# Carrying stores over a block's end, reloading split tokens from DRAM, and gathers in groups: a three-stage decoder layer on one core

## Chip, core and metric

The kernel runs on one core of a Trainium2 chip. The metric is device time in microseconds: the median of several executions of the kernel before is set against that of the changed kernel on the same chip. An execution with the profiler on is recorded beside them.

## What is computed

One decoder layer with three residual parts over x of 8 × 256 tokens with 256 channels, in float32.

```python
x = x + mamba2(layernorm(x))                # W_in: z, x: 4096 channels each (64 heads of 64), B, C: 128 each, dt: 64
x = x + cross_attention(layernorm(x), ctx)  # 16 heads of 128, 4 key heads, 64 context tokens, q and k RMS-normed
x = x + experts(layernorm(x))               # 8 experts of 640, 2 per token, and 2 shared ones

# mamba2: xBC = silu(conv4(x, B, C)); dt = softplus(dt + bias); dA = dt * A
#         y = scan(C, B, dA, x * dt) + D * x; return rmsnorm(y * silu(z)) * norm_w @ W_out.T
# experts: s = sigmoid(x @ router.T); the two largest of s, normalized to sum 1, weigh two of 8
#          w_e * (silu(x @ wg.T) * (x @ wu.T)) @ wd.T, and the shared experts are added unweighted
```

## The kernel before

The 2048 tokens are 16 tiles of 128, in 4 groups of 512. The large products are float32 operands split into a high part, rounded to the type that TensorE multiplies at full rate, and a low part that holds the rest; a product is three matmuls (high by high, low by high, high by low), so each tile of tokens and each weight needs a high part (a copy by ScalarE) and a low part (a subtraction by DVE or POOL).

The program is a row of blocks. In each the five engines run instruction lists written by hand, with semaphores between them; at a block's end all engines meet, and the next begins.

`mamba_prepare` (0 to 91 us of work): layer norm, transposes of x into the buffers called `pair` (`pair_hi`, `pair_lo`), dt, the decay sums, B and C with their convolution. Beside it the weights w_xz go through in 16 pieces j: SP loads a piece (512 KB), ScalarE makes the high part (`w_high(j)`), DVE (j < 7) or POOL the low part, SP stores both to DRAM (`w_split`, 1 MB). The parts lie in a ring of four buffers, so `w_high(j)` waits for the store of j − 4. The loop over the 8 tiles m of the B/C convolution carries `w_high` along:

```python
tanh(m)
if m + 9 < NJ:      # NJ = 16
    w_high(m + 9)
```

SP waits for all 16 stores before the block ends. The decay sums `a_by_head` are stored in four transfers behind piece 10. The first weights (`w_first`) and decays are already in place for the scan.

`mamba_scan` (97.6 to 967): 128 iterations, 4 groups of tokens by 32 tiles of channels. Each loads split weights again from DRAM, projects x and z (`x_proj`, `z_proj`, six matmuls of 128x512 each), and does the scan, the gate and the output projection for neighbouring iterations. At n = 8 SP issues the attention's loads.

`cross_attention_phase` (to 1282.8): 8 sequences b. Sequence b's scores, softmax (`exp` on ScalarE, the rest on DVE) and attend run beside the q projections of b + 1 (`q_pair` on TensorE, `q_out` on ScalarE: four ACTIVATEs which free the PSUM bank of the q_pair two further on), and beside layer norm, transposes, high and low parts (`f_high`, `f_low`; `x2_hi`, `x2_lo`) and router logits of b − 1. The parts of x2 are one pair of small buffers, used for the logits alone. `pair` holds wq's parts here.

`ffn_phase`: `dense(0)` is the first shared expert over all tokens: 4 units u of 512 tokens by 5 tiles of the hidden width, 20 steps k of `gate_up` (12 matmuls of 128x512), ScalarE's `silu`, DVE's `h` and its low part (`to_lo`), `down(u)`. Beside its steps runs the routing on DVE: `logits_in`, `scores`, `ranks`, ties, choices, at k = 5 TensorE's `counts_before`, then places; POOL scatters token rows by expert to DRAM in groups of 8 indirect transfers, each group waiting for the one before. `f_xT_hi`, `f_xT_lo` are the tokens' transposed parts again: `transposes`, `xT_high`, `xT_low` for 16 tiles, four ahead of the first gate_up, the last two tiles (14, 15, whose logits are made here by `late_logits`) at k = 0, the others at k = 2, 3, 7, 8 and 12. Then come 39 tiles of sorted rows (1390.6 to 1630), and `dense(1)`, the second shared expert, in which POOL gathers the results (32 indirect transfers, two a tile; a tile's buffer is free once an earlier tile is combined) and DVE's `combine(n)` adds tile n at the steps k = 4 to 19.

## Time and profile before

| | |
|---|---|
| median of the runs | 1717.1 us (3 runs, 1716.67 to 1723.58) |
| the recorded execution | 1731.19 us |
| its span | 1729.4 us, 28895 instructions |
| mean granted TensorE clock | 0.973 |
| TensorE busy (matmul) | 1614.9 us, 93% |
| DVE / ScalarE / POOL busy | 1311.0 / 1222.5 / 601.3 us |
| DMA | 220.30 MB, mean 127 GB/s |

Times of the trace are from the span's start. The recorded execution has 1.8 us outside its span. "Idle before" and its releaser stand in brackets behind an instruction. PE is TensorE, ACT ScalarE, SP the engine that issues most transfers. The prefixes p_, m_, a_ and f_ of names stand for the four stages.

### The profile page before, as it was taken

The numbers are of one execution on the slowest core, as the hardware profiler recorded it, in microseconds if no ns is written. First come the engines' busy times: TensorE is split into PE (matmuls) and PEld (weight loads), VectorE is DVE, ScalarE is ACT, GpSimd is POOL, SyncE is SP. The second block draws the span as 40 slices with busy tenths as digits, with TensorE's granted clock in tenths as the row PEclk, the third lists the DMA queues.
The fourth block names the chain that finished last, engine by engine and source line by source line (L and its number), as shares of the span: only waits on it lengthen the run. The fifth ranks groups of instructions, "written<-read, shape, count | busy, mean of one in ns | idle before, by whom it ended". The sixth has DMA issues, their size and how long they took to land. (4 is left out here: it accounts for less than half of the span.)

```text
span 1729.4 us, 28895 instructions
## 1 busy us (share of the span) xinstructions
PE 1614.9 (93%) x9892; PEld 1289.2 (75%) x9892; DVE 1311.0 (76%) x2048; ACT 1222.5 (71%) x2531; POOL 601.3 (35%) x469
## 2 busy tenths in 40 slices
PE   4479999999999999999999999999968999999989
PEld 3257777777777777777777677777757889999868
DVE  7859999999999999999999756765557533333345
ACT  5669999999999999999999566665524333444321
POOL 1413343434343434343433321111112563336450
PEclk9679999999999999999999999999979999999989
DMA  8956444444444444444442100000132323222221
GB/s 309 393 212 246 162 155 170 148 163 154 170 149 162 155 170 150 169 147 171 148 170 98 55 1 1 1 1 1 47 105 84 127 103 110 93 91 96 79 86 43
DMA packets 74268, 220.30 MB, mean 127 GB/s; under 512 B 8848, under 2 KB 29584, under 8 KB 72464
## 3 DMA queue, kind: packets, MB, share of 16 engines
q1 hardware_dynamic: 68464, 192.38, 31.1%
q0 software_dynamic: 5664, 26.09, 4.3%
q8 instruction: 84, 1.38, 0.3%
q14 instruction: 56, 0.46, 0.1%
HBM read 184.62 MB, written 33.82 MB: 126 GB/s over the span
## 5 line engine op out<-in xcount | busy, mean ns | idle before, releaser
L607 POOL TENSOR_TENSOR m_gT<-m_gy,m_zs 128x512 f32<-128x512 f32 x128 | 166.7, 1302 | 537.5 <-DVE m_gy L769 537.5
L728 DVE SCALAR_TENSOR_TENSOR m_xc<-banks,k_cw,m_xc 128x510 f32<-128x510 f32 (+2 forms) x384 | 285.4, 743 | 21.1 <-ACT m_xc L647 12.1
L868 PE MATMUL m_ps_out<-k_won,m_gT 128*128 128x256 f32 x1024 | 242.3, 379 | 3.6 <-POOL m_gT L607 2.0
L825 PE MATMUL banks<-pair_hi,m_wxz 128*128 128x512 f32 x680 | 243.8, 409 | 0.5 <-DMA m_wxz<-w_split 0.5
L740 DVE TENSOR_TENSOR m_mat<-m_mat,k_cbm 128x768 f32<-128x768 f32 x256 | 232.5, 950 | 2.0 <-ACT m_mat L668 2.0
L868 PEld LDWEIGHTS m_ps_out<-k_won,m_gT 128*128 128x128 f32 x1024 | 193.6, 189 | 36.6 <-POOL m_gT L607 3.3
L856 PE MATMUL m_ps_y<-m_mat,m_xdt 128*64 128x256 f32 (+1 forms) x2048 | 194.7, 332 | 0.0
L668 ACT ACTIVATE m_mat<-m_mat 128x1536 f32<-128x1536 f32 x128 | 188.5, 1473 | 0.1
L856 PEld LDWEIGHTS m_ps_y<-m_mat,m_xdt 128*64 128x64 f32 x2048 | 126.8, 136 | 80.0 <-issue 42.3
L659 ACT ACTIVATE m_mat<-m_a_all,k_cum 128x256 f32<-128x256 f32 x340 | 170.7, 502 | 0.0
L618 POOL TENSOR_TENSOR m_g_sum<-m_g_sum,m_g_sq 128x512 f32<-128x512 f32 x124 | 163.2, 1316 | 5.2 <-ACT m_g_sq L674 5.1
L825 PEld LDWEIGHTS banks<-pair_hi,m_wxz 128*128 128x128 f32 x680 | 128.8, 189 | 29.5 <-DMA m_wxz<-w_split 1.2
L2331 PE MATMUL f_gu<-f_room,f_gT_hi 128*128 x468 | 141.3, 363 | 2.4 <-issue 2.4
L2184 DVE TENSOR_TENSOR f_h<-f_silu,f_gu 128x256 f32<-128x256 f32 (+1 forms) x117 | 44.1, 377 | 129.4 <-PE f_ps_hT L2341 107.1
L825 PE MATMUL banks<-pair_lo,m_wxz 128*128 128x512 f32 x340 | 135.4, 398 | 0.0
L825 PE MATMUL banks<-pair_hi,k_w_first 128*128 128x512 f32 x344 | 127.2, 410 | 7.5 <-PEq L73 6.6
L661 ACT ACTIVATE m_mat<-m_a_all,k_cum 128x128 f32<-128x128 f32 x340 | 134.0, 394 | 0.0
L2254 PE MATMUL f_gu<-f_xT_hi,f_room 128*128 128x512 f32 x320 | 109.0, 415 | 11.8 <-ACT f_silu L1904 5.6
L647 ACT ACTIVATE m_xc<-banks,logits,k_cw 128x512 f32<-128x512 f32 x128 | 98.4, 768 | 13.2 <-PE banks L825 13.2
L1093 POOL TENSOR_TENSOR a_q_r<-a_q_ve,a_neg_half 128x32 f32<-128x32 f32 x8 | 43.4, 5429 | 176.8 <-DVE a_q_ve L1280 176.8
L1937 ACT ACTIVATE f_silu<-f_gu 128x256 f32<-128x256 f32 (+1 forms) x117 | 40.9, 349 | 88.0 <-PE f_gu L2331 88.0
L769 DVE SCALAR_TENSOR_TENSOR m_gy<-m_xs,logits,m_ps_y 128x512 f32<-128x512 f32 x128 | 95.5, 746 | 8.5 <-PE m_ps_y L856 0.2
(305 smaller groups left out, 3695.9 us busy)
## 6 DMA issues: line engine op xcount, KB each, us to landing
m_wxz<-w_split SPq DMA_DIRECT2D x85, 512.0 KB, 3.3
m_a_all<-a_by_head SPq DMA_DIRECT2D x85, 512.0 KB, 4.3
k_w_first<-w_split SPq DMA_DIRECT2D x43, 512.0 KB, 3.4
k_a_first<-a_by_head SPq DMA_DIRECT2D x43, 512.0 KB, 4.3
w_split<-p_w_hl SPq DMA_DIRECT2D x16, 1024.0 KB, 9.9
raw<-in_w_gate_up POOLq DMA_DIRECT2D x9, 1280.0 KB, 6.8
raw<-in_w_xz SPq DMA_DIRECT2D x16, 512.0 KB, 7.9
raw<-in_w_down POOLq DMA_DIRECT2D x9, 640.0 KB, 7.9
```

Of the source, the lines that this page charges most:

```text
L607: pool.tensor_tensor(gT[:, n % 2, :], gy[:, n % 2, :], zs[:, n % 2, :], ALU.mult).then_inc(g_done, 1)
L618: pool.tensor_tensor(g_sum[:, g % 2, :], g_sum[:, g % 2, :], g_sq[:, n % 2, :], ALU.add)\
L659: act.activation(mat[:, u, h, b * TRI:b * TRI + SEQ], a_all[u][:, h, b * SEQ:(b + 1) * SEQ], ACT.Relu, bias=cum[:, t, head:head + 1], scal ...
L661: last = act.activation(mat[:, u, h, b * TRI + SEQ:(b + 1) * TRI], a_all[u][:, h, b * SEQ + P:(b + 1) * SEQ], ACT.Relu, bias=cum[:, t + 1, ...
L668: act.activation(mat[:, n % 3], mat[:, n % 3], ACT.Exp, scale=-1.0).then_inc(exp_done, 1)
L728: dve.scalar_tensor_tensor(out=out[:, :, k:], in0=ps[:, :, 0:SEQ - k], scalar=cw[:, c, TAPS - 1 - k:TAPS - k], in1=out[:, :, k:], op0=ALU. ...
L740: dve.tensor_tensor(mat[:, u, h, :], mat[:, u, h, :], cbm[:, g * BG:(g + 1) * BG, :].rearrange("p b t -> p (b t)"), ALU.mult)\
L825: last = pe.matmul(ps[:, :], w, a, start=m == 0, stop=m == len(terms) - 1)
L856: last = pe.matmul(ps_y[h * HD:(h + 1) * HD, b * SEQ + at:(b + 1) * SEQ], xdt[:, 2 * b + half, h * HD:(h + 1) * HD], mat[:, u, h, b * TRI ...
L868: last = pe.matmul(ps_out[:, q * HID:(q + 1) * HID], gT[:, n % 2, q * P:(q + 1) * P], won[:, c, :], start=c == 0 and q % 2 == 0, stop=c == ...
L2254: last = pe.matmul(bank[n % 2][:, :], w, a, start=m == 0, stop=m == len(terms) - 1)
L2331: last = pe.matmul(ps_gu[m % 4][:, 0:2 * (i1 - i0)], a, w, start=q == 0, stop=q == len(terms) - 1)
```

## The change

1. `mamba_prepare`: the semaphores of the stores live on into the scan. The block's end waits for pieces 0 to 13; SP waits for the last two in the scan at n = 8, POOL before its first product. Piece 15 is split into a part of `raw`, and its high part waits for the low part of an earlier piece in place of a store. In the loop over m tanh(5) and tanh(6) stand ahead of `w_high(14)`, tanh(7) ahead of `w_high(15)`. The four stores of `a_by_head` go one each behind pieces 8 to 11; DVE's `w_low(0)` and `w_low(1)` come among the layer norm's tiles. At the scan's start `z_proj(0)` is ahead of `x_proj(1)`, `tanh_x` ahead of `decays`, `silu_x(0)` ahead of `matrices(0)`.
2. Attention: `q_out(b+1, 2)` is ahead of `exp(b, 0)`. The parts x2 of b = 0 to 5 are stored to DRAM (12 stores of 256 KB), those of b = 6 are written straight to `pair`, and after the last q_pair SP loads the stored ones into `pair` (2 × 1.5 MB). In the experts `pair` takes the place of `f_xT`; only tiles 14 and 15 are transposed there, TensorE and ScalarE wait for the reload, and `late_logits` stands behind the k = 1 gate_up.
3. Gathers: group g of 8 waits until group g − 1 has landed; the combines from tile 4 on come one step later, the last two together.

```diff
+        last_hl = raw[:, 0:2 * CH * XZ].bitcast(F32R).rearrange("p (c s m) -> p c s m", c=CH, s=2)
...
+        def hl(j):
+            if j == NJ - 1:
+                return last_hl
+            return w_hl[:, (0, 1, 3, 2)[j % RING]]
...
-                if j == NJ - 6:
+                if NJ - 8 <= j < NJ - 4:
                     sp.wait_ge(aT_done, 2)
-                    for q in range(TPG):
+                    for q in (j - NJ + 8,):
...
-            for u in range(RING):
-                sp.wait_ge(w_stored[u], 16 * len(range(u, NJ, RING)))
+            sp.wait_ge(w_stored[0], 16 * (NJ // RING))
+            sp.wait_ge(w_stored[1], 16 * (NJ // RING))
+            sp.wait_ge(w_stored[2], 16 * (NJ // RING - 1))
+            sp.wait_ge(w_stored[3], 16 * (NJ // RING - 1))
...
-                if j >= RING:
+                if j == NJ - 1:
+                    act.wait_ge(w_lo_pool, NJ - 2 - LOW)
+                elif j >= RING:
                     act.wait_ge(w_stored[j % RING], 16 * (j // RING))
-                act.activation(w_hl[:, j % RING, :, 0, :], w_raw[:, j % RING], ACT.Copy).then_inc(w_hi_done, 1)
+                act.activation(hl(j)[:, :, 0, :], w_raw[:, j % RING], ACT.Copy).then_inc(w_hi_done, 1)
...
-                if m + 9 < NJ:
+                if m + 9 < NJ - 2:
                     w_high(m + 9)
+                elif m == NM - 2:
+                    w_high(NJ - 2)
+            w_high(NJ - 1)
...
+                if n == 11:
+                    w_low(0)
+                if n == NT - 1:
+                    w_low(1)
...
-            w_low(0)
-            w_low(1)
...
                 if n == 8:
+                    sp.wait_ge(w_stored[2], 16 * (NCT // 8))
+                    sp.wait_ge(w_stored[3], 16 * (NCT // 8))
...
+            pool.wait_ge(w_stored[2], 16 * (NCT // 8))
             for n in range(N):
...
             scale_x(0)
-            for n in range(2):
-                gaps(n, 0)
-                gaps(n, 1)
-                decays(n)
-                if n == 0:
-                    tanh_x(0)
-                    tanh_z(0)
-            for n in range(N):
+            gaps(0, 0)
+            gaps(0, 1)
+            tanh_x(0)
+            decays(0)
+            tanh_z(0)
+            scale_x(1)
+            gaps(1, 0)
+            gaps(1, 1)
+            tanh_x(1)
+            decays(1)
+            tanh_z(1)
+            gaps(2, 0)
+            gaps(2, 1)
+            decays(2)
+            for n in range(1, N):
...
             conv_x(0)
+            silu_x(0)
             matrices(0)
-            silu_x(0)
...
             x_proj(0)
+            z_proj(0)
             x_proj(1)
-            z_proj(0)
...
+        kept = (NB - 2) * TT
+        x2_dram = nc.dram_tensor("x2_parts", [2, P, KK, kept], F32, kind="Internal").ap()
...
+        def x2_parts(b):
+            if b < NB - 2:
+                return x2_hi[:], x2_lo[:]
+            return wq_hi[:, :, b * TT:(b + 1) * TT], wq_lo[:, :, b * TT:(b + 1) * TT]
...
+            def x2_store(b):
+                sp.wait_ge(f_lo_done, b + 1)
+                for n, part in enumerate(x2_parts(b)):
+                    sp.dma_start(x2_dram[n, :, :, b * TT:(b + 1) * TT], part.bitcast(F32)).then_inc(x2_stored, 16)
+
+            for b in range(NB - 3):
+                x2_store(b)
             sp.wait_ge(vw_ready, NP * HP)
             for dst, src, loaded in next_weights:
                 sp.dma_start(dst, src).then_inc(loaded, 16)
+            x2_store(NB - 3)
+            sp.wait_ge(x2_stored, 32 * (NB - 2))
+            sp.wait_ge(q_ready, NB * HP)
+            for n, part in enumerate(wq_parts):
+                sp.dma_start(part[:, :, 0:kept].bitcast(F32), x2_dram[n]).then_inc(x2_loaded, 16)
...
             def f_high(b):
                 act.wait_ge(f_T_ready, b + 1)
-                if b >= 1:
+                if b == NB - 2:
+                    act.wait_ge(q_ready, NB * HP)
+                elif b >= 1:
                     act.wait_ge(logits_ready, b)
-                act.activation(x2_hi[:].rearrange("p k (q t) -> p q k t", q=TB),
+                    act.wait_ge(x2_stored, 32 * b)
+                act.activation(x2_parts(b)[0].rearrange("p k (q t) -> p q k t", q=TB),
...
                     q_out(b + 1, 1)
+                    q_out(b + 1, 2)
                 exp(b, 0)
                 if more:
-                    q_out(b + 1, 2)
                     q_out(b + 1, 3)
...
-    ORDER = [*range(TPG), *range(DONE, NT), *range(TPG, DONE)]
-    UNIT_READY = [TPG, 2 * TPG + LATE, 3 * TPG + LATE, NT]
-    TURN = {2: TPG + LATE, 3: TPG + LATE + 2, 7: 2 * TPG + LATE, 8: 2 * TPG + LATE + 2, 12: 3 * TPG + LATE}
+    COMBINED = [*([t] for t in range(TPG)), [], *([t] for t in range(TPG, NT - 2)), [NT - 2, NT - 1]]
...
             for n in range(NT):
+                if n and n % TPG == 0:
+                    pool.wait_ge(gathered[n // TPG - 1], 16 * TOP * TPG)
                 if n >= NT // TOP:
...
-            xT_high(0)
-            xT_high(1)
-            act.wait_ge(weights_loaded, 32)
+            act.wait_ge(inputs_loaded, 64)
             part_high(0)
-            xT_high(2)
-            xT_high(3)
             part_high(1)
...
-            xT_low(0)
-            xT_low(1)
             part_low(0)
-            xT_low(2)
-            xT_low(3)
+            part_low(1)
             dve.wait_ge(ln_rstd, 1)
             for n in range(DONE, NT):
                 dve.tensor_scalar(xn[:, n, :], xres[:, n, :], mv[:, n - DONE, 0:1], rstd[:, n - DONE:n - DONE + 1],
                                   ALU.subtract, ALU.mult).then_inc(normed, 1)
-            part_low(1)
-            xT_low(TPG)
-            xT_low(TPG + 1)
             part_low(2)
+            xT_low(0)
+            xT_low(1)
...
                         if d == 1 and k >= HT - NT:
-                            combine(k - HT + NT)
+                            for t in COMBINED[k - HT + NT]:
+                                combine(t)
...
-                    if d == 0:
-                        pe.wait_ge(xT_lo_done, UNIT_READY[u])
+                    if d == 0 and u == 0:
+                        pe.wait_ge(inputs_loaded, 64)
+                    if d == 0 and u == UNITS - 1:
+                        pe.wait_ge(xT_lo_done, LATE)
...
                         if d == 0 and k == 0:
-                            transposes(TPG)
-                            transposes(TPG + 1)
+                            transposes(0)
+                            transposes(1)
+                        if d == 0 and k == 1:
                             late_logits()
-                        if d == 0 and k in TURN:
-                            transposes(TURN[k])
-                            transposes(TURN[k] + 1)
                         if d == 0 and k == IT:
                             counts_before()
 
```

The end of the first stage on ScalarE: `p_w_hl<-raw` is w_high, `banks<-p_xc` tanh, `p_xc<-banks` the convolution's scaling. Before:

```order
42 L259 ACTIVATE banks<-p_xc 128x512
43 L247 ACTIVATE p_w_hl<-raw 128x2x512
44 L254 ACTIVATE p_xc<-banks,logits,k_cw 128x512
45 L259 ACTIVATE banks<-p_xc 128x512
46 L247 ACTIVATE p_w_hl<-raw 128x2x512
47 L259 ACTIVATE banks<-p_xc 128x512
48 L247 ACTIVATE p_w_hl<-raw 128x2x512
49 L259 ACTIVATE banks<-p_xc 128x512
```

and with the change, where L257, L269 and L264 are the same three lines:

```order
42 L269 ACTIVATE banks<-p_xc 128x512
43 L257 ACTIVATE p_w_hl<-raw 128x2x512
44 L264 ACTIVATE p_xc<-banks,logits,k_cw 128x512
45 L269 ACTIVATE banks<-p_xc 128x512 x2
46 L257 ACTIVATE p_w_hl<-raw 128x2x512
47 L269 ACTIVATE banks<-p_xc 128x512
48 L257 ACTIVATE raw<-raw 128x2x512
```

Two tanh now stand together in front of w_high(14), and the last w_high, whose output is `raw`, is behind the last tanh.

The attention on ScalarE around `exp(b, 0)` of one sequence (L1159; L1132 and L1133 are a q_out's steps). Before:

```order
1813 L1132 ACTIVATE a_qT<-a_ps_q1,a_bq 128x256
1814 L1133 ACTIVATE a_q_sq<-a_ps_q1,a_bq 128x256
1815 L1132 ACTIVATE a_qT<-a_ps_q1,a_bq 128x256
1816 L1133 ACTIVATE a_q_sq<-a_ps_q1,a_bq 128x256
1817 L1159 ACTIVATE a_s<-a_s 128x1024
1818 L1132 ACTIVATE a_qT<-a_ps_q0,a_bq 128x256
1819 L1133 ACTIVATE a_q_sq<-a_ps_q0,a_bq 128x256
1820 L1132 ACTIVATE a_qT<-a_ps_q0,a_bq 128x256
1821 L1133 ACTIVATE a_q_sq<-a_ps_q0,a_bq 128x256
1822 L1132 ACTIVATE a_qT<-a_ps_q1,a_bq 128x256
```

and with the change (exp is L1209, q_out L1182 and L1183):

```order
1812 L1182 ACTIVATE a_qT<-a_ps_q1,a_bq 128x256
1813 L1183 ACTIVATE a_q_sq<-a_ps_q1,a_bq 128x256
1814 L1182 ACTIVATE a_qT<-a_ps_q1,a_bq 128x256
1815 L1183 ACTIVATE a_q_sq<-a_ps_q1,a_bq 128x256
1816 L1182 ACTIVATE a_qT<-a_ps_q0,a_bq 128x256
1817 L1183 ACTIVATE a_q_sq<-a_ps_q0,a_bq 128x256
1818 L1182 ACTIVATE a_qT<-a_ps_q0,a_bq 128x256
1819 L1183 ACTIVATE a_q_sq<-a_ps_q0,a_bq 128x256
1820 L1209 ACTIVATE a_s<-a_s 128x1024
1821 L1182 ACTIVATE a_qT<-a_ps_q1,a_bq 128x256
```

One q_out, four rows on the bank a_ps_q0, moved from behind exp to ahead of it.

The experts' routing on DVE from the copy of the late logits on (L2021 and L2022 late logits, L2128 h, L2107 to_lo, L1987 xT_low, L1975 part of the weights, L2026 to L2034 routing). Before:

```order
1353 L2021 COPY logits<-f_ps_hT 128x16
1354 L2022 TENSOR_SCALAR logits<-logits 128x128
1355 L2128 TENSOR_TENSOR f_h<-f_silu,f_gu3 128x512
1356 L2107 TENSOR_TENSOR f_room<-f_h,f_room 128x512
1357 L1975 TENSOR_TENSOR f_room<-raw,f_room 128x4x128
1358 L2026 TENSOR_SCALAR logits<-logits 128x128
1359 L2028 RECIPROCAL logits<-logits 128x128
1360 L2128 TENSOR_TENSOR f_h<-f_silu,f_gu2 128x512
1361 L2107 TENSOR_TENSOR f_room<-f_h,f_room 128x512
1362 L1987 TENSOR_TENSOR f_xT_lo<-f_ps_gT,f_xT_hi 128x2x128
1363 L1987 TENSOR_TENSOR f_xT_lo<-f_ps_y,f_xT_hi 128x2x128
1364 L2033 TENSOR_TENSOR f_xg<-logits 128x1024
```

and with the change (late logits L2064 and L2065, h L2171, to_lo L2150, part of the weights L2022, routing L2069 to L2077):

```order
1350 L2064 COPY logits<-f_ps_hT 128x16
1351 L2065 TENSOR_SCALAR logits<-logits 128x128
1352 L2171 TENSOR_TENSOR f_h<-f_silu,f_gu3 128x512
1353 L2150 TENSOR_TENSOR f_room<-f_h,f_room 128x512
1354 L2022 TENSOR_TENSOR f_room<-raw,f_room 128x4x128
1355 L2069 TENSOR_SCALAR logits<-logits 128x128
1356 L2071 RECIPROCAL logits<-logits 128x128
1357 L2171 TENSOR_TENSOR f_h<-f_silu,f_gu2 128x512
1358 L2150 TENSOR_TENSOR f_room<-f_h,f_room 128x512
1359 L2076 TENSOR_TENSOR f_xg<-logits 128x1024
1360 L2077 TENSOR_TENSOR f_y<-logits 128x1024
1361 L2171 TENSOR_TENSOR f_h<-f_silu,f_gu3 128x512
```

The rows of xT_low between the routing's rows are gone; the order is otherwise the same.

## Rows read from the trace of the kernel before

**Rows 1.** Windows, the attention's stretch; columns: span, busy (xcount) per engine, PEclk, DMA share, GB/s

```profile
967.00:1282.80 315.80, 291.85 (x1986) 227.66 (x1984) 197.27 (x328) 186.47 (x428) 61.52 (x46) 0.98 0.04 15
```

**Rows 2.** Timeline, PE, end of the first stage and scan's start; columns: start, us, instruction, idle before

```profile
97.60 0.76 PE L825 MATMUL banks<-pair_hi,k_w_first 128*128 128x512 f32 x1 [6.60 <-PEq L73]
...
101.01 0.79 PE L825 MATMUL banks<-pair_hi,m_wxz 128*128 128x512 f32 x1 [0.52 <-DMA m_wxz<-w_split]
```

**Rows 3.** Timeline, ACT, end of the first stage

```profile
85.75 1.06 ACT L247 ACTIVATE p_w_hl<-raw 128x1024 fp32r<-128x1024 f32 x1 [3.79 <-DMA w_split<-p_w_hl]
```

**Rows 4.** Timeline, DVE, end of the first stage

```profile
82.59 1.01 DVE L375 TENSOR_TENSOR k_cbm<-p_ps_cum,p_mask 128x384 f32<-128x384 f32 x2
87.32 0.69 DVE L370 SCALAR_TENSOR_TENSOR xn_ffn<-banks,p_xc 128x512 f32<-128x512 f32 x1 [3.72 <-ACT banks L259]
...
91.04 0.56 DVE L375 TENSOR_TENSOR k_cbm<-p_ps_cum,p_mask 128x384 f32<-128x384 f32 x1 [0.72 <-PE p_ps_cum L468]
```

**Rows 5.** Timeline, SP's DMA issues, end of the first stage

```profile
77.25 3.49 SPq L176 DMA_DIRECT2D w_split<-p_w_hl  x3
...
83.93 5.69 SPq L176 DMA_DIRECT2D w_split<-p_w_hl  x2
```

**Rows 6.** DMA view of 60 to 98 us: 40 slices in GB/s; issues, KB each, us to landing

```profile
GB/s 367 392 431 423 414 427 414 423 423 418 414 418 436 418 418 398 356 228 121 118 259 412 411 423 427 423 414 410 397 397 375 418 414 418 431 332 82 47 13 0
...
w_split<-p_w_hl SPq DMA_DIRECT2D x8, 1024.0 KB, 11.0
```

**Rows 7.** Waits of PE, 1036 to 1282 us: total us, times, longest

```profile
PE a_ps_q L1440 <- ACT a_q_sq L1133: 9.2, 12, 1.2
```

**Rows 8.** Timeline, ACT, around one exp in the attention

```profile
1042.52 1.06 ACT L1159 ACTIVATE a_s<-a_s 128x1024 f32<-128x1024 f32 x1 [1.87 <-DVE a_s L1304]
1043.48 0.46 ACT L1132 ACTIVATE a_qT<-a_ps_q,a_bq 128x256 f32<-128x256 f32 x1
```

**Rows 9.** Timeline, PE, the same stretch

```profile
1045.09 0.38 PE L1440 MATMUL a_ps_q<-a_xT_hi,pair_hi 128*128 128x256 f32 x1 [1.24 <-ACT a_q_sq L1133]
...
1048.07 1.04 PE L1521 MATMUL banks<-ident,a_s 128*128 128x128 f32 x8
```

**Rows 10.** Timeline, DVE, the same stretch: the softmax's last step

```profile
1045.50 1.23 DVE L1311 TENSOR_TENSOR a_s<-a_s,a_s_sum 128x1024 f32<-128x1024 f32 x1
```

**Rows 11.** Timeline, PE, start of the experts' block

```profile
1286.05 0.50 PE L2254 MATMUL f_gu<-f_xT_hi,f_room 128*128 128x512 f32 x1 [0.96 <-DVE f_xT_lo L1987]
...
1292.14 0.27 PE L2226 MATMUL f_ps_hT<-wr_hi,f_xT_hi 128*128 128x8 f32 x1 [1.04 <-DVE f_xT_lo L1987]
...
1305.48 0.44 PE L2216 MATMUL f_ps_gT<-ident,xn_ffn 128*128 128x128 f32 x2 [1.46 <-DVE f_xT_lo L1987]
...
1315.88 0.49 PE L2297 MATMUL f_ps_hT<-f_both,f_below 128*128 128x128 f32 x2 [2.68 <-DVE f_first L2044]
```

**Rows 12.** Timeline, DVE, the same stretch

```profile
1298.81 3.42 DVE L2107 TENSOR_TENSOR f_room<-f_h,f_room 128x512 fp32r<-128x512 f32 x1
...
1305.01 0.42 DVE L1987 TENSOR_TENSOR f_xT_lo<-f_ps_gT,f_xT_hi 128x256 fp32r<-128x256 f32 x1
1305.34 0.41 DVE L1987 TENSOR_TENSOR f_xT_lo<-f_ps_y,f_xT_hi 128x256 fp32r<-128x256 f32 x1
```

**Rows 13.** Chain that ended last, from 1630 us: the pieces without a known releaser

```profile
1642.74 3.21 another core or an unknown queue
...
1648.23 11.15 another core or an unknown queue
```

**Rows 14.** Timeline, POOL, gathers of the second pass

```profile
1633.77 1.02 POOL L1855 DMA_INDIRECT xn_ffn<-y_sorted,f_place  x1 [15.69 <-DMA y_sorted<-f_y]
...
1686.56 1.10 POOL L1855 DMA_INDIRECT xn_ffn<-y_sorted,f_place  x1 [0.31 <-issue]
```

**Rows 15.** Timeline, POOL, scatters: the first one behind a wait

```profile
1341.04 0.96 POOL L1831 DMA_INDIRECT x_sorted<-xn_ffn,f_place  x1 [1.71 <-DMA x_sorted<-xn_ffn,f_place]
```

**Rows 16.** Waits of ACT, 1340 to 1390 us: total us, times, longest

```profile
ACT f_silu L1904 <- remote: 17.5, 4, 13.4
```

More of the change, by code:

```diff
@@ L116, in mamba_prepare @@
             sem(n) for n in ("wdt_loaded", "wbc_loaded", "small_loaded", "wo_loaded"))
-        w_loaded, w_stored = ([sem(f"{n}{u}") for u in range(RING)] for n in ("w_loaded", "w_stored"))
+        w_loaded = [sem(f"w_loaded{u}") for u in range(RING)]
         w_hi_done, w_lo_dve, w_lo_pool, a_stored = (
@@ L935, in mamba_phase @@
         first = (sb("w_first", [P, 2, 2, KK, P], F32R)[:], sb("a_first", [P, 2, TG])[:],
[L936 removed]
+                 ctx.enter_context(nc.semaphore("w_first_loaded")), ctx.enter_context(nc.semaphore("a_first_loaded")),
+                 [ctx.enter_context(nc.semaphore(f"w_stored{u}")) for u in range(4)])
         retired = mamba_prepare(nc, xres, ident, raw, banks, scratch, kept, first, x, w_xz, w_bc, w_dt, conv_w, conv_b, dt_bias, a_log,
@@ L2137, in dense @@
                             scores()
-                        if d == 0 and k in TURN:
-                            xT_low(TURN[k])
-                            xT_low(TURN[k] + 1)
                         if d == 0 and k == 2:
@@ L2227, in late_logits @@
                 last.then_inc(logits_ready, 1)
-            for i in range(TPG):
-                transposes(i)
             def dense(d):
@@ L2406, in decoder_layer @@
             ctx.enter_context(nc.semaphore(n)) for n in ("ctx_loaded", "k_ready", "wq_copied", "wq_split"))
+        pair = [ctx.enter_context(nc.sbuf_tensor(n, [P, KK, TOK], F32R)) for n in ("pair_hi", "pair_lo")]
         with ExitStack() as front:
-            pair = [front.enter_context(nc.sbuf_tensor(n, [P, KK, TOK], F32R)) for n in ("pair_hi", "pair_lo")]
             banks = front.enter_context(nc.psum_tensor("banks", [P, 4 * TG], F32))
@@ L2415, in decoder_layer @@
                         d_param, norm_w, w_out)
-            cross_attention_phase(nc, xres, ident[:], raw, banks, xn_ffn, logits, wr_parts, pair, k_ready, wq_split,
-                                  [(gate_up_raw, w_gate_up[0], expert_loaded), (down_raw, w_down[0], expert_loaded)],
+            cross_attention_phase(nc, xres, ident[:], raw, banks, xn_ffn, logits, wr_parts, pair, ffn_loaded, k_ready, wq_split,
+                                  [(gate_up_raw, w_gate_up[0], ffn_loaded), (down_raw, w_down[0], ffn_loaded)],
                                   router_w, mask, bq, bv, wo, qn, kn)
-        ffn_phase(nc, xres, ident[:], raw, xn_ffn, logits[:], wr_parts, expert_loaded, w_gate_up, w_down, out)
+        ffn_phase(nc, xres, ident[:], raw, xn_ffn, pair, logits[:], wr_parts, ffn_loaded, w_gate_up, w_down, out)
 def lay_out(i):
```

73 lines of the change are left out of this document (35 added, 38 removed).

## The prediction

> **What bounds the kernel now.** I read the windows by stage first: in the attention's 315.8 us TensorE is busy for 291.9 at a granted clock of 0.98, the DMA engines for 0.04 [rows 1]. A stage like that is only shortened where TensorE waits or where matmuls go. So I went on to TensorE's short waits and to the seams between the blocks.
>
> The **first seam**: the scan's first matmul starts at 97.60 after 6.60 us idle, released by TensorE's own sequencer [rows 2], that is by the meeting of all engines at the block's end. DVE ends at 91.60 [rows 4], SP issues its last store at about 89.6 [rows 5] and waits for it; the 1 MB stores of this stretch land 11.0 us after issue (median) [rows 6]. So the last landings set the block's end. They are late because ScalarE's last split waits 3.79 us for an older store out of the same buffer [rows 3], and tanh(7) stands behind it, so that DVE sits 3.72 us in front of silu(7) [rows 4].
>
> The **attention**: TensorE waits 12 times, 9.2 us in all, for a q_out of ScalarE [rows 7]; six of these are of about 1.25 us, as at 1045.09 [rows 9]. Just before it ScalarE is idle for 1.87 us in front of exp, waiting for DVE's scores, with the q_out that TensorE needs queued behind exp [rows 8].
>
> The **experts' start**: gate_up begins at 1286.05, behind four tiles' transposes; up to the counts at 1315.88 TensorE waits 1.04, 1.46 and 2.68 us, among others [rows 11]. DVE, in the low part of h at 1298.81, works on from there with the low parts of further tiles between its routing steps [rows 12].
>
> **The recorded execution** took 1731.2 us, its span 1729.4, so it is 14.1 above the median of the runs, 1717.1. Its chain has two pieces "another core or an unknown queue", 3.21 and 11.15 us, 14.4 together [rows 13], in the shared expert's second pass, where ScalarE and DVE stand still for a cause that the profile does not name. The amounts agree, so I take these pieces to be what this execution has above the timed ones: differences from its rows go on 1717.1, and the pieces are not to be won there.
>
> **The change, part by part.** *First seam.* With tanh(5) and tanh(6) ahead of w_high(14) and tanh(7) ahead of w_high(15), silu(7) can start when the masks before it end, 83.6, in place of 87.32; the 4.28 us from there to DVE's end stay [rows 4]: 87.9. The block's end waits for pieces 12 and 13 instead of 14 and 15; SP issues them in the row from 77.25 [rows 5], and with 11.0 us under way [rows 6] they land at 88 to 91. I take 90.0 for the first matmul, −7.6. Ends: 88.4 with the computation alone (−9.2), 93 if the landings are as late as now against the issue (−4.6). *The scan's first load.* The next weights landed 3.4 us behind the first matmul, a wait of 0.52 [rows 2]. Now 2 MB of left stores are ahead of them: at 415 GB/s [rows 6] 5 us, so they land near 5.5. But z_proj(0), six matmuls on weights that are there already, moves ahead of x_proj(1), and TensorE asks for them at 5.5 to 6 in place of 2.9. I take +0.5 for this and the re-ordered first period together (0 to +3). This is where a rule speaks against the change: the Trainium skill, "DMA: Bandwidth & Descriptors", section "Queues, rings and completion order", says that each DMA engine consumes the descriptors of SP's queue in ring order, so that a load at the scan's start cannot pass the stores left behind. By that rule, without z_proj in between, the sum would be some 2.5 us worse. The new waits at n = 8 and before POOL's first product come after the stores have landed. Seam **−7.1** (−9 to −2).
>
> *Attention.* TensorE's wait ends at 1045.09, 1.6 us after that q_out's start at 1043.48 [rows 8, 9]: about what fits into the 1.87 us idle, so exp is hardly later. TensorE then comes to the probabilities (1048.07 now) 1.2 us earlier, at 1046.8; DVE finishes them at 1046.73 [rows 10]. That leaves no slack, so I take 6 × 1.17 = **−7.0** (−8; −3 if softmax is late by more than half of it). The stores of the split parts, 12 of 256 KB, and the reload of 3 MB have idle DMA engines: at 415 GB/s the reload takes 8 us, it is issued when the last q_pair is done, some 35 us before the block's end. Cost 0; without that cover it would be 8 us in front of gate_up.
>
> *Experts.* Fourteen of 16 tiles come without transposes and splits. gate_up starts when part 0 of the weights is split, 1284.6 by the rows' durations, −1.45. Then the counts hang on DVE's chain. h(1), which stands just ahead of the row at 1298.81, comes earlier by 1.45 and the late logits' wait of 1.04 [rows 11], but stands behind their copy, which moved behind k = 1: −2.0. Two pairs of xT_low of 0.7 leave the chain [rows 12], −1.3. The split of h took 3.42 us, where 128x512 takes 0.7 elsewhere; of that excess I take −0.7 (0 to −2.7). Counts −4.0. TensorE's own waits and transposes fall by more than that, so it waits longer for the counts than now. Behind the counts three pairs of transposes go; a row of 0.44 is half of a pair [rows 11], the rows overlap, and I take 0.42 a pair, −1.3. **−5.3** (−8 to −3).
>
> *Gathers.* They are 1.25 us apart (0.95 and 0.30 idle); the last is issued at 1686.56 and no combine waits for it [rows 14]. Now group g is issued behind the landing of g−1. In the scatter, which is paced so already, such a wait took 1.71 us [rows 15]. From 1633.8 on the last group would be out at 1633.8 + 4 × 10 + 3L for a landing time of L: 1679 with L = 1.71, and up to L = 4.2 ahead of what the buffers allow anyway. **0.**
>
> Sum −7.1 − 7.0 − 5.3 = −19.4: 1697.7; a recorded execution would show 1711.8 with the unnamed pieces and 1697 without.
>
> **The rivals.** (a) *The unnamed stall belongs to the gathers, and to the timed runs too.* For: it lies where up to 18 gathers are out, and pacing leaves 8. Against: in the paced scatter ScalarE has a like wait, 13.4 us [rows 16]. Were some 12 us of it in the timed runs, and gone: 1685.7; 15%. The Trainium skill, "Runtime: NRT & Kernel Launch", section "Instruction fetch mechanics", has instruction blocks fetched by a DMA queue, mostly hidden; no row here ties the stall to it. (b) *The gains run into second chains*: the left stores cost the scan 3 us (−4), softmax is late (−3), DVE's long split stays and something takes its room (−4): 1706; 17%. (c) *Little comes through*: the backlog of the DMA engines sets the first matmul (−2), DVE bounds the attention (0), experts −3: 1712; 5%. (d) *Slower, by the gathers.* Each us of L above 4.2 delays the last group by three: break-even at L = 10.7, slower by 0.5% from 13.6 on, against 1.71 seen; at 14 it gives 1727; 3%.
>
> **How the numbers follow.** The forecast has 60%, with a range of its own of 1691 to 1704. The whole range adds (a) and most of (b): 1684 to 1707. A measurement of this kernel tells about 0.5%, 8.6 us, so faster is below 1708.5: the forecast, (a) and (b), 0.92. Same is (c), 0.05; slower is (d), 0.03.
>
> **What would show it.** The scan's first matmul at 90 ± 1.5, with less than 2 us of wait for its first load; no wait of 1.2 us of the q_pairs for a q_out and 1.1 us less per sequence; from the experts' first gate_up to the counts 27.3 us (29.8 now) and no wait for the reload; the gathers in groups of 8 with gaps near 1.7. Wrong would be: a first matmul at 93 or later, an attention of unchanged length, a wait for the reload, a combine behind a gather, or timed runs at 1686, where only (a) leads.

## The result and the profile after

| | before | changed |
|---|---|---|
| median of the runs | 1717.83 us (4 runs) | 1703.32 us (4 runs) |
| range | 1716.67 to 1723.58 | 1702.16 to 1704.77 |
| ratio, 95% interval | | 0.9906 (0.9889 to 0.9922) |
| recorded execution / its span | 1731.19 / 1729.4 | 1703.08 / 1701.3 |
| mean granted clock | 0.973 | 0.980 |

The change is 14.5 us faster by the medians. The forecast was 1697.7, −19.4 us, with a range of 1684 to 1707. The recorded executions differ by 28.1 us, twice as much as the runs: the one of before carries the unnamed pieces.

So that no such piece disturbs the reading, both kernels were recorded again in one comparison on one chip (`before_2`, `whole_2` below). Starts of the stages in those two, in us:

| | before | changed | gained since the row above |
|---|---|---|---|
| scan's first matmul | 97.33 | 90.13 | 7.2 |
| attention's first matmul | 969.24 | 961.13 | 0.9 |
| experts' block, first DVE instruction | 1285.28 | 1267.84 | 9.3 |
| first gate_up of the sorted tiles | 1389.76 | 1372.66 | −0.3 |
| first gate_up of the second pass | 1629.52 | 1612.47 | 0.0 |
| end of the span | 1716.1 | 1700.6 | −1.6 |

Each gain belongs to the stage that ends at its row: 9.3 is the attention's, −0.3 that of the experts' start. The seam gained what was said and the attention somewhat more. The experts' start gained nothing, and the shared expert's second pass became longer. Now the rows, first the changed kernel's timeline of TensorE at the scan's start, against [rows 2]; columns as there:

```profile
89.73 0.48 PE L850 MATMUL banks<-pair_hi,k_w_first 128*128 128x512 f32 x1 [2.52 <-PEq L73]
...
96.95 0.49 PE L850 MATMUL banks<-pair_hi,m_wxz 128*128 128x512 f32 x1 [3.03 <-DMA m_wxz<-w_split]
```

The first matmul came at 89.73 (90.0 said), the wait in front of it is 2.52 in place of 6.60. The wait for the first load is 3.03, where 0.52 stood and under 2 was said. SP's issues in the same stretch, against [rows 5]:

```profile
84.71 1.04 SPq L182 DMA_DIRECT2D w_split<-p_w_hl  x1
87.52 0.36 SPq L182 DMA_DIRECT2D w_split<-raw  x1
89.85 0.33 SPq L602 DMA_DIRECT2D m_wxz<-w_split  x1
```

The stores left behind are issued at 84.71 and 87.52 and land 8.4 and 8.1 us later, at 93.1 and 95.6; the first load, issued at 89.85, lands behind them, 7.1 us later, at 96.95. The same load took 3.3 us in the kernel before. The Trainium skill, "DMA: Bandwidth & Descriptors", section "Queues, rings and completion order", states that each DMA engine consumes a queue's descriptors in ring order, though a later write may finish before an earlier one. The order of the three landings agrees with it, but does not prove it: a load that merely shared the busy DMA engines with the stores would be late too, and no run tells the two apart. DVE's end of the first stage, against [rows 4]:

```profile
84.89 0.68 DVE L385 SCALAR_TENSOR_TENSOR xn_ffn<-banks,p_xc 128x512 f32<-128x512 f32 x1
86.59 1.21 DVE L390 TENSOR_TENSOR k_cbm<-p_ps_cum,p_mask 128x384 f32<-128x384 f32 x2 [1.01 <-PE p_ps_cum L483]
```

silu(7) starts at 84.89 in place of 87.32 and waits for nothing, and DVE ends at 87.80 (87.9 said, 91.60 before). The sum came out by two errors that cancel: silu(7) was said for 83.6, and the 4.28 us from there to DVE's end were said to stay, where they are 2.91.

The attention, waits of TensorE from 960 to 1268 us (total us, times, longest), against [rows 7]:

```profile
PE a_ps_q L1494 <- ACT a_q_sq L1183: 2.8, 10, 0.3
```

The six waits of 1.25 us are gone; those of 0.3 are left. (Over the whole stage, which is longer than the stretch of [rows 7], the kernel before has 16 such waits, 10.5 us.) Then the experts' start (the first line is its first gate_up, the second the counts, the third gT(0), the transposes of the first sorted tile, the last that tile's gate_up), TensorE's timeline against [rows 11]:

```profile
1269.54 0.47 PE L2291 MATMUL f_gu<-pair_hi,f_room 128*128 128x512 f32 x1 [2.55 <-DVE f_room L2022]
...
1293.71 0.80 PE L2332 MATMUL f_ps_hT<-f_both,f_below 128*128 128x128 f32 x2 [4.63 <-DVE f_first L2087]
...
1365.61 0.69 PE L2340 MATMUL f_ps_gT<-ident,f_xg 128*128 128x128 f32 x2 [4.15 <-DMA f_xg<-x_sorted]
...
1373.44 0.49 PE L2366 MATMUL f_gu<-f_room,f_gT_hi 128*128 x1 [1.34 <-issue]
```

gate_up begins 1.77 us after DVE's first instruction of the block at 1267.77 (3.24 before), and the counts stand at 1293.71, 24.2 us behind that gate_up (27.3 said). The term up to the counts held; the sign came out lower because the 29.8 us of the recorded execution of before held some 3 us of slow clock: it is 26.7 in `before_2`, 24.2 in `whole_2`. But TensorE now waits 4.63 us for the counts (2.68 before), and a wait appears that the recorded execution of before did not have: 4.15 us for the sorted rows in front of gT(0). The chain that ended last, from 1300 us, in order of time:

```profile
1308.53 1.29 POOL x_sorted L1883
...
1355.71 2.41 DMA x_sorted<-xn_ffn,f_place
1358.14 7.42 DMA f_xg<-x_sorted
1365.61 0.69 PE f_ps_gT L2340 x2
1366.30 5.81 PE f_ps_hT L2315 x30
```

and the scatters it stands on, on POOL:

```profile
1308.53 1.29 POOL L1883 DMA_INDIRECT x_sorted<-xn_ffn,f_place  x1 [24.83 <-DVE f_place L2121]
...
1320.48 0.96 POOL L1883 DMA_INDIRECT x_sorted<-xn_ffn,f_place  x1 [1.72 <-DMA x_sorted<-xn_ffn,f_place]
...
1334.28 0.96 POOL L1883 DMA_INDIRECT x_sorted<-xn_ffn,f_place  x1 [3.52 <-DMA x_sorted<-xn_ffn,f_place]
...
1346.06 1.29 POOL L1883 DMA_INDIRECT x_sorted<-xn_ffn,f_place  x1 [1.71 <-DMA x_sorted<-xn_ffn,f_place]
```

The end of the stage hangs on: places ready, 32 scatters of about 1.26 us each with three waits between groups, a load of sorted rows that lands 7.4 us later, the first tile. In the second pass the gathers now go in groups of 8, and the waits between the groups are 2.01, 1.99 and 2.21 us (1.7 said); the first:

```profile
1628.65 1.19 POOL L1909 DMA_INDIRECT xn_ffn<-y_sorted,f_place  x1 [2.01 <-DMA xn_ffn<-y_sorted,f_place]
```

No combine waits for a gather. Last the second pass on TensorE, the chain of the changed kernel from 1608 us:

```profile
1613.25 27.99 PE f_gu L2291 x120
1641.24 7.20 PE f_ps_hT L2315 x60
1648.43 13.99 PE f_gu L2291 x60
1662.43 7.20 PE f_ps_hT L2315 x60
1669.62 13.99 PE f_gu L2291 x60
1683.61 14.40 PE f_ps_hT L2315 x120
```

No unnamed piece is in it; TensorE works through. The same chain of the kernel before in `before_2`:

```profile
1629.52 27.23 PE f_gu L2254 x120
1656.74 7.19 PE f_ps_hT L2280 x60
1663.94 13.63 PE f_gu L2254 x60
```

Sixty gate_up matmuls take 13.99 us where 13.63 stood, and there are 240 in each pass: 1.5 of the 1.6 us lost there.

### The profile page after: what moved, and what is told of

Same layout as the page of the kernel before. It is cut to its first block and busy times, and to the rows that moved or that the text cites. A ratio compares the mean times of both kernels' runs of the same rounds, so it can differ in the third digit from the quotient of the medians.

```text
span 1701.3 us, 28825 instructions
## 1 busy us (share of the span) xinstructions
PE 1609.6 (95%) x9864; PEld 1286.1 (76%) x9864; DVE 1306.2 (77%) x2034; ACT 1217.4 (72%) x2517; POOL 600.7 (35%) x469
## 5 line engine op out<-in xcount | busy, mean ns | idle before, releaser
L2291 PE MATMUL f_gu<-pair_hi,f_room 128*128 128x512 f32 x320 | 104.5, 403 | 3.0 <-DVE f_room L2022 2.5
```

What stands on the lines that cost most here:

```text
L2291: last = pe.matmul(bank[n % 2][:, :], w, a, start=m == 0, stop=m == len(terms) - 1)
```

## The experiments

In each comparison the kernel before ran beside the others on the same chip. Its median there was 1729.7, 1720.4 and 1719.7 us; so kernels are compared inside a comparison only.

### The parts alone, and the change without the pacing

`seam_alone` is the kernel before with the first part of the change (all of its hunks up to `mamba_scan`, and the semaphores handed on). `qout_alone`:

```diff
                     q_out(b + 1, 1)
+                    q_out(b + 1, 2)
                 exp(b, 0)
                 if more:
-                    q_out(b + 1, 2)
                     q_out(b + 1, 3)
```

`experts_alone` is the changed kernel with the hunks of the seam, the q_out move and the pacing taken back. `no_pacing` is the changed kernel with

```diff
-    COMBINED = [*([t] for t in range(TPG)), [], *([t] for t in range(TPG, NT - 2)), [NT - 2, NT - 1]]
+    COMBINED = [[t] for t in range(NT)]
...
-                if n and n % TPG == 0:
-                    pool.wait_ge(gathered[n // TPG - 1], 16 * TOP * TPG)
```

Expected of `seam_alone`: 

> The kernel before with the first part of the change alone (stores carried over the block's end, the order at the scan's start). By the two traces the scan's steady period and the attention's start come 7.5 us earlier with the whole change, so: -7.5 us against the kernel before, first matmul of the scan near 89.7. Rival (the gain of this part is partly due to something later): less than -5.

Expected of `qout_alone`: 

> The kernel before with q_out(b+1,2) ahead of exp(b,0) and nothing else. The attention of the changed kernel is 7.6 us shorter; if that is all this move, -7.6 us here; if the stores of x2 or the merged POOL steps had a share, the number is smaller. The forecast said -7.0.

Expected of `experts_alone`: 

> The kernel before with the x2 parts stored and reloaded and the experts' transposes gone, without the seam, the q_out move and the pacing. Theory A (the chain counts, places, 32 scatters, reload of sorted rows sets the first tile, and eats what TensorE gained): the counts come 7 us earlier against the block's start, but the whole gains at most 1 us; TensorE waits some 4 us for f_xg before gT(0). Rival B (the forecast's step: the gain at the counts goes through): -5.3 us.

Expected of `no_pacing`: 

> The changed kernel without the gathers' groups (no wait for the group before, combines at their old steps). Theory A: the unnamed pieces were in one recorded execution alone: same time as the changed kernel, 1703 +- 1. Rival: pacing keeps the stall away in timed runs too: 10 us or more slower than the changed kernel, and the stall is back in the profile.

| kernel | median | range | ratio to before (95%) |
|---|---|---|---|
| before | 1729.66 | 1725.24 to 1732.46 | |
| seam_alone | 1723.02 | 1719.13 to 1725.02 | 0.9959 (0.9942 to 0.9976) |
| qout_alone | 1720.83 | 1714.98 to 1721.81 | 0.9945 (0.9924 to 0.9967) |
| experts_alone | 1726.09 | 1722.58 to 1733.5 | 0.9985 (0.9971 to 1.0) |
| no_pacing | 1712.94 | 1710.91 to 1717.32 | 0.9900 (0.9883 to 0.9918) |

The seam alone gives 6.6 us and the q_out move 8.8; the intervals, 4.2 to 10.0 and 5.7 to 13.1 us, hold the 7.5 and 7.6 expected. No other part of the change is needed for these two: with the q_out move alone the attention takes 306.8 us, as with the whole change. For the experts the timed runs do not decide. They give 3.6 us by the medians, more than the 1 us of theory A and less than the 5.3 of theory B, in runs that spread over 11 us. Their interval reaches from 0 to 5.0, so it leaves out B's 5.3 only narrowly; and as the second pass loses 1.5 us in this kernel, B's gain in the stage would show as 3.8. What speaks for theory A is the rest: the two other parts alone add up to 15.5 of the 16.7 us that `no_pacing` gains, the stage takes 106.0 us in the profile against 106.2 and 107.1 in those of `seam_alone` and `qout_alone`, and the profile has the wait in front of gT(0), on TensorE:

```profile
1383.91 0.69 PE L2312 MATMUL f_ps_gT<-ident,f_xg 128*128 128x128 f32 x2 [2.99 <-DMA f_xg<-x_sorted]
```

All four recorded executions of this comparison had second passes of 97 to 100 us, 10 to 13 us longer than the undisturbed ones of their kind, with waits that have no known releaser. In `no_pacing` the chain holds one such piece:

```profile
1634.54 10.38 another core or an unknown queue
```

and its median lies 10 us above what the changed kernel had beside its own kernel before (1703.3, in the table of the result). Against the kernel before in its own comparison, though, its ratio is that of the changed kernel, 0.990. So this could be the pacing or the occasion, and nothing was decided yet.

### The changed kernel again, the pacing alone, the places earlier, the last store later

`pacing_alone` puts the group wait and `COMBINED` into the kernel before. `places_spots_early`, on the changed kernel:

```diff
-                        if d == 0 and k == IT + 1:
+                        if d == 0 and k == IT:
                             so_far = places()
-                        if d == 0 and k == IT + 2:
                             spots(so_far)
```

`store15_late`, on the changed kernel; `last_parts` is the part of `raw` that holds piece 15:

```diff
 # mamba_prepare, SP
+                if j < NJ - 1:
                     sp.dma_start(w_dram[j * CH:(j + 1) * CH]...
 # mamba_scan, SP, behind the loads of n
+                if n == 2:
+                    sp.dma_start(w_dram[NCT - 2:NCT].rearrange("c p m -> p c m"),
+                                 last_parts).then_inc(w_stored[3], 16)
```

Expected of `whole`: 

> The changed kernel unaltered, beside the kernel before on this chip, whose runs in the last comparison were 1725 to 1732 where the first ones were 1717 to 1724. Theory C (the unnamed stall of some 10 us is in the timed runs on some chips or at some times, and pacing removes it): on a chip where before takes 1729, this takes 1703 again, 1.5% faster. Theory A (pacing does nothing): 1713, like the kernel without pacing.

Expected of `pacing_alone`: 

> The kernel before with the gathers' groups and the moved combines alone. Theory C: -8 to -12 us where before takes 1729, no piece without a known releaser over 3 us in the second pass; about 0 where before takes 1717. Theory A: 0 on either.

Expected of `places_spots_early`: 

> The changed kernel with DVE's places and spots right behind h(5) and the choices' counts, in place of behind h(6) and h(7). DVE waits 5.1 us for TensorE there. Theory A of the experts (the chain counts, places, scatters, reload sets the first tile): the scatters start about 7 us earlier, the wait of 4.1 us for f_xg before gT(0) and the half clock behind it (2.4 us) go: -5 to -6.5 us against the changed kernel, 1697 or so. Rival (the chain has nothing to do with it, the 4 us are a slow transfer): the wait stays, 0.

Expected of `store15_late`: 

> The changed kernel with the last 1 MB store issued by SP in the scan, behind the loads of n = 1 and 2, in place of at the first block's end. If the first load of the scan waits in SP's queue behind the left stores (3.0 us at x_proj(1), landing 7.1 us after issue), it lands 2.5 us earlier and 1 to 2.5 us are gained against the changed kernel; if DVE's chain of the first period sets the scan's start anyway, the wait shrinks but the steady period comes no earlier: 0.

| kernel | median | range | ratio to before (95%) |
|---|---|---|---|
| before | 1720.37 | 1716.02 to 1722.2 | |
| whole | 1702.89 | 1701.67 to 1703.52 | 0.9901 (0.9882 to 0.992) |
| pacing_alone | 1719.26 | 1715.9 to 1723.19 | 1.0001 (0.9988 to 1.0013) |
| places_spots_early | 1696.78 | 1695.19 to 1699.5 | 0.9871 (0.985 to 0.9892) |
| store15_late | 1704.36 | 1703.38 to 1705.23 | 0.991 (0.9891 to 0.9929) |

**Places.** Starting the chain earlier gives 6.1 us more, inside the 5 to 6.5 expected. TensorE's rows:

```profile
1292.71 0.80 PE L2331 MATMUL f_ps_hT<-f_both,f_below 128*128 128x128 f32 x2 [4.63 <-DVE f_first L2087]
...
1365.51 0.49 PE L2365 MATMUL f_gu<-f_room,f_gT_hi 128*128 x1 [1.34 <-issue]
```

and POOL's first scatter:

```profile
1300.12 1.29 POOL L1883 DMA_INDIRECT x_sorted<-xn_ffn,f_place  x1 [17.44 <-DVE f_place L2121]
```

The scatters start 7.4 us behind the counts in place of 14.8, the wait of 4.15 us in front of gT(0) is not there any more, and the first tile's gate_up comes 72.8 us behind the counts in place of 79.7. In the changed kernel DVE is idle for 5.12 us at just this place:

```profile
1299.98 0.69 DVE L2171 TENSOR_TENSOR f_h<-f_silu,f_gu 128x512 f32<-128x512 f32 x1 [5.12 <-PE f_gu L2291]
```

The granted clock behind the counts is the lower one here too (0.80 us for the first pair of rows in both), but DVE no longer waits there before the places. This version beats both kernels: 1696.8 against 1702.9 and 1720.4 in one comparison. The move was not run on the kernel before. There TensorE waits 1.5 to 3.2 us for the sorted rows in four recorded executions, so the 6.1 us are probably the two calls and the transposes together, and not the calls alone.

**The last store.** TensorE has no wait for its first load any more, and nothing is gained: 1.5 us slower by the medians. Both kernels' second transposes of the scan come at the same time. `store15_late`, TensorE:

```profile
108.37 1.11 PE L873 MATMUL banks<-ident,m_xs 128*128 128x128 f32 x4 [4.19 <-DVE m_xs L775]
```

the same, DVE:

```profile
105.88 1.83 DVE L769 TENSOR_TENSOR m_mat<-m_mat,k_cbm 128x768 f32<-128x768 f32 x2 [2.07 <-ACT m_mat L690]
```

and `whole`, TensorE:

```profile
97.22 0.59 PE L850 MATMUL banks<-pair_hi,m_wxz 128*128 128x512 f32 x1 [2.80 <-DMA m_wxz<-w_split]
...
108.30 1.12 PE L869 MATMUL banks<-ident,m_xs 128*128 128x128 f32 x4 [3.16 <-DVE m_xs L771]
```

The wait for the load (2.80) has become a longer wait for DVE (4.19 for 3.16), and DVE in turn waits 2.07 us for ScalarE's matrices. The scan's start is set by the chain ScalarE, DVE, and most of the late load hides beside it. Most, because the two executions did not begin alike: in `store15_late` the scan's first matmuls ran at the lower clock, and its first DVE instruction came 1.03 us later (93.92 against 92.89). In `whole` DVE does wait once behind the load, for transposes of TensorE:

```profile
100.83 0.69 DVE L784 TENSOR_TENSOR m_xdt<-banks,k_dt 128x512 f32<-128x512 f32 x1 [0.87 <-PE banks L869]
```

So the late load cost at most about 0.9 us here (an estimate from this wait), and the comparison does not show that it cost nothing.

**The pacing** alone gives nothing where the kernel before takes 1720.

### Pacing and stores once more, on one chip

Expected of `whole_2`: 

> The changed kernel again, as the measure for the next two on one chip. 1.5% under the kernel before, wherever that lies; the second pass of the shared expert (from the last tile to the span's end) 88 us as in both of its recorded executions.

Expected of `no_pacing_2`: 

> The changed kernel without the gathers' groups again, now on one chip with the changed kernel; so far the paced kernels' second pass was 87 to 88 us and the unpaced ones' 97 to 100, but on different chips, whose times for the kernel before differ by 9 us. Theory C (pacing removes the stall everywhere): 8 to 12 us over the changed kernel, second pass 97 or more. Theory D (the stall and the 9 us belong to the chip, pacing does nothing): within 2 us of the changed kernel, second passes alike.

Expected of `before_2`: 

> The kernel before unaltered, for its profile on this chip: theory C wants a second pass of 97 us or more, with pieces without a known releaser of some 14 us; theory D the same second pass as the changed kernel's, about 87, if this chip's time for it is near 1718.

`all_waited` is the changed kernel with

```diff
-            sp.wait_ge(w_stored[2], 16 * (NJ // RING - 1))
-            sp.wait_ge(w_stored[3], 16 * (NJ // RING - 1))
+            sp.wait_ge(w_stored[2], 16 * (NJ // RING))
+            sp.wait_ge(w_stored[3], 16 * (NJ // RING))
```

Expected: 

> The changed kernel, but the first block's end waits for all 16 stores again; the orders on ScalarE and the rest of the seam stay. The last two stores were issued at 84.7 and 87.5 and stores took 8 to 10 us: first matmul of the scan at 96 to 97 in place of 89.8; its first load is then alone in the queue, so the 3.0 us wait goes: +3.5 to +4.5 us against the changed kernel. Rival (ScalarE's new order alone brought the gain, the stores land anyway): 0.

| kernel | median | range | ratio to before (95%) |
|---|---|---|---|
| before (before_2 is one more run, 1717.86) | 1719.74 | 1717.0 to 1722.12 | |
| whole_2 | 1703.69 | 1702.32 to 1703.84 | 0.9908 (0.9891 to 0.9924) |
| no_pacing_2 | 1705.49 | 1703.19 to 1705.87 | 0.9914 (0.9898 to 0.9931) |
| all_waited | 1711.48 | 1711.23 to 1712.0 | 0.9952 (0.9935 to 0.9969) |

**Pacing.** Without it the kernel is 1.8 us slower by the medians, the intervals overlap, and the second pass is 88.2 us with and without. The kernel before has a second pass of 86.6 us without an unnamed piece. In `pacing_alone`, whose x stands where it stood before, the second pass is 86.7 us. Theory D was right on the main point, pacing does little when there is no stall, but wrong in tying the stall to a chip: the first and the third comparison of these experiments ran on the same chip, and the kernel before took 1729.7 in one and 1719.7 in the other. So the stall comes and goes on one chip. Of the seven executions recorded without pacing five have it (the first of the kernel before, and the four of the first comparison), of the seven with pacing none; but no paced kernel ran in the comparison where it was in all four. Whether pacing would have kept it away stays open. Its cause does too. A late fetch of instructions is not what the traces show: in none of the five stalls do the trace's two instruction queues move a packet.

**Stores.** Waiting for all stores costs 7.8 us, more than the 3.5 to 4.5 I expected:

```profile
96.18 0.77 PE L850 MATMUL banks<-pair_hi,k_w_first 128*128 128x512 f32 x1 [8.60 <-PEq L73]
...
114.39 1.11 PE L869 MATMUL banks<-ident,m_xs 128*128 128x128 f32 x4 [4.21 <-DVE m_xs L771]
```

The first matmul is 6.05 us later than in `whole_2` (90.13), as expected, and the wait for the first load is gone; but that wait had been all but free, so nothing comes back for it: the second transposes of the scan come 6.1 us later than in `whole` (114.39 against 108.30). The other 1.7 of the 7.8 us are not explained. ScalarE's new order with the old wait brings only 1.2 us of the 7.2 (96.18 against 97.33): most of the gain needs the stores left to run over the block's end. It needs the order too, since DVE ended at 91.60 in the old one, later than the new first matmul; the left stores without the order were not run.

**Why the experts' start gains nothing.** From the block's first DVE instruction to the first gate_up of the sorted tiles the five recorded executions with the transposes take 103.9 to 107.8 us, 105.9 on average, the eight without them (and with the places where they were) 104.8 to 106.3, on average 105.6. With one of each kind, both recorded undisturbed, the steps can be set side by side, in us from the block's first DVE instruction: counts at 29.9 before and 26.0 changed, −3.9. From the counts to the first scatter 12.75 and 14.47, +1.7. From there to the load of sorted rows 48.1 and 49.6, +1.5, with a group wait of 3.56 where the others are 1.7. (This second group wait is 2.1 to 3.8 us in all eight and 1.7 in all five; why is open.) From the load to gT(0) 7.1 and 6.8, −0.3. From gT(0) to the first tile 6.6 and 7.9, +1.3, at a granted clock of 0.78 and 0.63. Sum +0.3. The windows behind the counts show the second of these (columns as in [rows 1]); `before_2`, then `whole_2`:

```profile
1315.20:1320.00 4.80, 4.80 (x23) 4.08 (x24) 2.39 (x5) 1.12 (x2) 0.00 (x0) 1.00 0.00 0
```

```profile
1293.80:1300.00 6.20, 6.19 (x19) 5.09 (x20) 1.42 (x3) 1.11 (x2) 0.00 (x0) 0.59 0.00 0
```

TensorE is busy throughout in both, but the granted clock is 1.00 before and 0.59 in the changed kernel, a mixture of its two levels, 2.4 and 1.2 GHz, after a wait of 4.63 us in place of 2.67. gate_up(6) so takes longer, DVE waits for it 4.78 us with h(6), and the places stand behind h(6). And in `before_2` TensorE already waits for the sorted rows, as it does in `pacing_alone` (3.15 us), `seam_alone` (2.31) and `qout_alone` (1.51):

```profile
1383.15 0.69 PE L2305 MATMUL f_ps_gT<-ident,f_xg 128*128 128x128 f32 x2 [2.55 <-DMA f_xg<-x_sorted]
...
1389.76 0.49 PE L2331 MATMUL f_gu<-f_room,f_gT_hi 128*128 x1 [1.34 <-issue]
```

The kernel before was at this bound too. In its first recorded execution the stage had a stall of 1.92 us on TensorE and a slow clock at the start (0.73 over 1286 to 1295), and they covered the wait.

## Why the prediction came out as it did

**Right: the seam.** −7.1 was said, −7.5 up to the attention in the first two recorded executions, −6.6 alone. The first matmul (90.0, 89.73) and the cause, the stores, held. DVE's end (87.9 said, 87.8) came by luck, by two errors of 1.3 and 1.4 us against each other. The part on the load was right in its sum and wrong in its reason: the load came 7.2 us behind the first matmul, not 5.5, TensorE asked for it after 4.2, not 5.5 to 6, so z_proj did not cover it; what hid most of it was DVE's chain. "With less than 2 us of wait" was missed.

**Right: the attention.** −7.0 was said, with "no slack" behind it; the stage is 7.6 us shorter in the first two recorded executions, 9.3 in the second two, and 8.8 us by `qout_alone`. Over all recorded executions it takes 314.9 to 316.0 us without the move (five) and 306.7 to 307.6 with it (nine), 8.3 less. The cause is the one said, the waits for the q_out: over the whole stage they fall from 10.5 to 2.8 us, 7.7, of which the prediction had counted the six long ones. The other 0.6 us are open. The stores and the reload cost nothing: `qout_alone`, which has neither, has the same attention (306.8), and TensorE's first gate_up waits for DVE's weights, not for the reload.

**Wrong: the experts, −5.3.** This is the step that failed. The two sums up to the counts were good: −1.45 (−1.47), and counts −4.0 (−3.9 between the undisturbed ones). One of their parts was not: of DVE's long instruction −0.7 was taken, and it stays, 3.43 us in `before_2` and 3.35 in the changed kernel, both times beside a subtraction of POOL of about 3 us; h(1) came earlier by more than said and made up for it.

```profile
1278.04 3.35 DVE L2150 TENSOR_TENSOR f_room<-f_h,f_room 128x512 fp32r<-128x512 f32 x1
```

What failed is that the sum, beyond the counts, only took TensorE's transposes away. I carried a gain at the counts through to the end of the stage and added the transposes taken out of TensorE's list behind it, without following places, scatters and the load of sorted rows to gT(0). That chain takes about 70 us, TensorE's own list to gT(0) about as much, and it ended last; the stage became 0.3 us longer in place of 5.3 shorter. The rows that show it are in the trace of before: the scatters are there with their group waits [rows 15], and their start hangs on DVE's place. I had read them for the pacing alone. Also, I wrote that TensorE "waits longer for the counts than now" as if a longer wait were free; the rows behind it are at the lower clock, and DVE's places came later for it.

**Not seen: the shared expert's matmuls.** In the second pass, for which I had only the gathers, they cost 1.5 us: sixty take 13.99 us in every recorded kernel that reads x from `pair` and 13.63 in every other, with and without pacing. The first pass has the same two rates (three matmuls in 0.70 us against 0.68).

**Right so far: the gathers, 0.** Without a stall pacing gives nothing one can measure, and the groups' waits of 2.0 to 2.2 us are far from the 4.2 at which they would cost something. The reading of the recorded execution, that it lay 14 us above the timed ones by the unnamed pieces and that these are not to be won, fits `before_2`, which has none of them and takes 1717.9. Rival (a) was not what happened: in the two undisturbed executions the whole gain is that of the seam, the scan and the attention, 7.2 + 0.9 + 9.3, less 1.9 for the rest, 15.5 us.

The sum, −19.4 said: between the two undisturbed executions 5.3 for the experts did not come and 0.3 was lost there, 1.6 was lost in the second pass, and the attention did 2.3 and the seam with the scan 1.0 better than said: −15.5. By the medians of the three comparisons that timed the changed kernel it is −14.5, −17.5 and −16.1. That the time lies inside the range is in part luck: a term of 5.3 us was missing, and two others were better than said.

## What to carry to other kernels

Follow a gain to the next place where all chains meet, not to the next wait: a term is only worth what the chain that ends last there gives up, and work taken from an engine that isn't in that chain gives nothing until the chain is shortened too. Where an engine goes idle in front of a step while the step that others need stands behind it in its list, look at the order first: 14 tiles' transposes taken out, with DRAM stores and a reload, gave nothing in this stage by themselves, and 6.1 us came once the places were moved by one and two steps. And one recorded execution can hold a stall that timed runs don't; record the kernel before twice before its rows are subtracted from.

## What was not expected of the hardware

- A gate_up matmul of 128x512 takes 233 ns (13.99 us for 60) where x comes from `pair`, and 227 ns (13.63 for 60) where it came from `f_xT`, both at a granted clock of 1.00, on the same chip. So it is in all recorded executions, nine with `pair` and five with `f_xT`. The layout within a partition is the same; the place of the buffers in the memory, of the weights' too, is not. Which of these it is wasn't tried.
- The unnamed stalls come and go on one chip, in the second pass above all: four recorded executions of one comparison had second passes 10 to 13 us too long, and of four in a later comparison on the same chip none had, two of them without pacing. The instruction queues moved no packet in any of the five stalls recorded.
- After a wait of 4.6 us for the counts the granted clock behind it was 0.59 over 6.2 us (`whole_2`); after 2.7 us it was 1.00 (`before_2`). The first rows behind the counts are at the lower level in all nine executions with the long wait, at the higher one in all five with the short. Elsewhere the length of the wait does not decide it: the scan's first matmul is at the higher level after 3.30 us (`whole_2`) and at the lower one after 0.93 (`places_spots_early`), and from gT(0) to the first tile the clock is 0.78 after 2.55 us (`before_2`) and 1.00 after 3.15 (`pacing_alone`):

```profile
1382.57 0.44 PE L2309 MATMUL f_ps_gT<-ident,f_xg 128*128 128x128 f32 x2 [3.15 <-DMA f_xg<-x_sorted]
```
